# fp8 attention of an eight-layer kernel: k, v and q projected apart, and another order on TensorE, ScalarE and VectorE

## The chip, the cores and the metric

One core of a Trainium2 chip. Its engines run their own instruction streams in order and meet through semaphores: TensorE (PE: matmuls and transposes, results in PSUM), ScalarE (ACT: functions, copies out of PSUM), VectorE (DVE: elementwise work and reductions), GpSimd (POOL, which works in SBUF here) and SyncE (SP, which issues the transfers). The metric is the device time of one execution in microseconds; lower is better.

## The reference, cut to what matters

The model is four pairs of a gated attention and a gated feed-forward layer on x (8 batches, 128 tokens, 256 features), with a context of the same shape. The change touches the second attention, `L1_xattn`: 16 query heads and 8 key heads of 128, once over the tokens and once over the context.

```python
ln_out = _ln(hidden_states, ln_w, ln_b)
q = _fp8_linear_pertensor(ln_out, wq, wq_scale, q_in_scale).reshape(b, s, g, hpg, d)
q = _ln(q, qln_w, qln_b)
k = _fp8_linear_pertensor(ln_out, wk, wk_scale, k_in_scale).reshape(b, s, g, d)
k = _ln(k, kln_w, kln_b)
v = _fp8_linear_pertensor(ln_out, wv, wv_scale, v_in_scale).reshape(b, s, g, d)
core = _gqa(q, k, v).reshape(b, s, nh * d)
qx = _fp8_linear_pertensor(ln_out, wqx, wqx_scale, qx_in_scale).reshape(b, s, g, hpg, d)
qx = _ln(qx, qxln_w, qxln_b)
kvx = jnp.einsum('bsi,oi->bso', cond, w_kv_x)
kx, vx = jnp.split(kvx, 2, axis=-1)
kx = _ln(kx.reshape(b, sc, g, d), kxln_w, kxln_b)
xout = _gqa(qx, kx, vx.reshape(b, sc, g, d)).reshape(b, s, nh * d)
catq = _div_clamp_fp8(jnp.concatenate([core, xout], axis=-1), proj_smooth)
return jnp.einsum('bsi,oi->bso', catq, wproj) * (proj_in_scale * proj_w_scale)
```

`_fp8_linear_pertensor` divides its input by a scale for each feature, clamps it, rounds it to fp8 and multiplies by the weights; `_gqa` is softmax(q k / sqrt(128)) v.

## The kernel before

The program runs the eight layers one after the other, each as one stream of instructions per engine. x stays in SBUF. The stage of interest (names that begin with C_) works on two batches at a time (g = 0, 1) in four steps. A **unit** is one batch and one of eight rounds r; a round is four query heads, rounds 0 to 3 over the tokens, 4 to 7 over the context. The 16 units of a step are u = 2 r + g. Two rounds share four key heads, so the units with u % 4 = 0 or 1 bring k and v (`brings_kv`). For r < 4 k and v come from the quantised input with weights split in two f16 parts (`project_split`, 4 matmuls of 512 columns), for r >= 4 from the context in f32 (`project`, 2 matmuls, each issued as two). q is always split.

The work is laid out by hand as a pipeline of **slots**: `C_slots` emits for slot n, for each entry (lag, stage) of an engine's list in the order of that list, that stage of unit n - lag, and then `extra`. `C_pipeline` emits slots 0 to 5, a hardware loop over three steps of slots 6 to 21, and once more slots 6 to 21, of which those from 16 on only finish units. Slots 16 to 21 of a step already take units 0 to 5 of the next one. The lists at L1214, L1251, L1324 and L1447 are the order of each engine.

What the stages of a unit do, in the order of its data:

- TensorE `projections`: k and v where due, then q, each into its own bank of PSUM (KBANK, VBANK, QBANK). k waits until the previous k is normalised (C_kn), v until the previous one is copied (C_v), q until the previous q is normalised (C_qn).
- ScalarE `squares_k`, `squares_q` (four squares with a sum each, then `variance` at L1267); GpSimd `deviations` (a power, L1227); VectorE `normed_k`, `normed_q` (L1153, L1158).
- TensorE `turn_k`, `turn_q` (four transposes each, both into TBANK, so they alternate with the copies `k_T`, `q_T` of ScalarE).
- TensorE `scores`, which wait for q's copy and for the previous exponentials (one bank, SBANK); VectorE `largest` (L1164); ScalarE `exps` (L1312); VectorE `probabilities` (L1171, L1172); TensorE `turn_p`; ScalarE `p_T` (L1318).
- ScalarE `v_out` copies v out of VBANK; TensorE `weigh` multiplies v by the turned p (L1424), after VectorE has read the previous result.
- VectorE `rounded` (L1180 to L1182, rounding to fp8 by L1113 to L1115), GpSimd `unshifted` (L1238), TensorE `out` (output projection, L1436).

Beside the units, `extra` of VectorE carries the inputs of the next step: `activations` quantises one batch's normalised input for one of four uses (n = 0 q, 1 qx, 2 k, 3 v; L1142 to L1146 and L1113 to L1120), in slots 11 to 16 and in 17 and 18; `norm_stats`, `again`, `twice_normed` in slots 6, 7 and 8 normalise the next two batches. TensorE turns them at the end of slot 10. A flag is a semaphore whose value says how many units have passed; `follow` takes over the semaphore of an earlier stage, where it stopped.

Of the kernel before, what the change touches and what calls it, by code (L numbers as in the profile page):

```python
# [29 lines left out]
G = 2  # L30
# [55 lines left out]
def program(nc, t, out, layers=8):  # L86

    with ExitStack() as ctx:
# [35 lines left out]
        ctxT = sb("ctxT", [P, G, KC, P])  # L124
# [462 lines left out]
        B_had = flag("B_had")  # L587
# [344 lines left out]
        C_vq = flag("C_vq", ROUNDS)  # L932
# [189 lines left out]
        def C_vector(dve, ch):  # L1122
# [61 lines left out]
            def extra(ch, i, n):  # L1184
                if n == UNITS + DEPTH - 1:
                    dve.wait_ge(C_out.sem, C_out.at(i))
                    for g in range(G):
                        add_to_x(dve, ch, i * G + g, PS[:, OUTBANK, g * D:(g + 1) * D], out_scale[:])
                if last_step(i):
                    return  # L1190
                if 1 <= n % UNITS <= G:
                    activations(ch, n % UNITS - 1, 1)
                if n == DEPTH:
                    norm_stats(ch, i + 1)
                if n == DEPTH + 1:
                    again(ch, i + 1)
                if n == DEPTH + 2:
                    twice_normed(ch, i + 1)
                if 11 <= n < 17:
                    m, g = divmod(n - 11, G)  # L1200
                    if m == 0:
                        dve.wait_ge(xT_ready.sem, xT_ready.at(i + 1, g))
                    activations(ch, g, (2, 3, 0)[m])
# [10 lines left out]
            C_pipeline(dve, ch, first, [(2, largest), (3, probabilities), (5, rounded), (0, normed_k), (0, normed_q)], extra)  # L1214
# [38 lines left out]
        def C_scalar(act, ch):  # L1253
# [25 lines left out]
            def squares_q(ch, i, u):  # L1279
                g, r = unit(u)  # L1280
                act.wait_ge(C_vq.sem, C_vq.nth(i, u))
# [5 lines left out]
            def v_out(ch, i, u):  # L1287
                if brings_kv(u):
                    g, r = unit(u)
                    nc.scalar.activation(flat(C_[g]["v"][:, (r // 2) % 2]), PS[:, VBANK, :], ACT.Copy,  # L1290
# [33 lines left out]
            C_pipeline(act, ch, lambda ch: feature_major(0), [(0, squares_k), (0, squares_q), (2, exps), (1, k_T), (0, v_out), (1, q_T), (3, p_T)],  # L1324
                       extra)

        def C_tensor(pe):
# [22 lines left out]
            def projections(ch, i, u):  # L1350
                g, r = unit(u)
                cross, quad, half = r // 4, (r // 2) % 2, r % 2
                x_of = lambda n: (lambda k: C_[g]["xs"][:, n, k, :])
                ctx_of = lambda k: ctxT[:, g, k, :]
                if r == 0:
                    pe.wait_ge(C_xs.sem, C_xs.nth(i, 8 * (u // UNITS) + 4 + g))
                if r == 4:
                    pe.wait_ge(C_xs.sem, C_xs.nth(i, 6 + g))
                    ctx_loaded(pe, i, g)
                if half == 0:  # L1360
                    if u:
                        pe.wait_ge(C_kn.sem, C_kn.nth(i, kv_at(u) - 1))
                        pe.wait_ge(C_v.sem, C_v.nth(i, kv_at(u) - 1))
                    if u == 12 and not last_step(i):
                        pe.wait_ge(xT_ready.sem, xT_ready.at(i + 1, G - 1))
                    if cross:
                        project(KBANK, ctx_of, wC["kx"], 512 * quad).then_inc(C_k.sem, 1)
                        last = project(VBANK, ctx_of, wC["vx"], 512 * quad)
                        if quad:
                            last.then_inc(ctx_read[g], 1)  # L1370
                    else:
                        project_split(KBANK, x_of(2), "k", 512 * quad).then_inc(C_k.sem, 1)
                        project_split(VBANK, x_of(3), "v", 512 * quad)
                if u:
                    pe.wait_ge(C_qn.sem, C_qn.nth(i, u - 1))
                project_split(QBANK, x_of(cross), "qx" if cross else "q", 1024 * quad + 512 * half).then_inc(C_vq.sem, 1)
# [65 lines left out]
            def extra(ch, i, n):  # L1442
                if n == 10 and not last_step(i):
# [4 lines left out]
                       [(2, scores), (0, projections), (1, turn_k), (3, turn_p), (6, out), (1, turn_q), (4, weigh)], extra)  # L1448
# [1531 lines left out]
```

## Time and profile before

| | us |
|---|---|
| median of 3 runs | 1937.25 |
| lowest, highest | 1935.76, 1951.46 |
| profiled execution | 1931.56 |
| its span, first to last instruction | 1929.8 |
| TensorE, VectorE, ScalarE, GpSimd busy | 1464.8, 1213.7, 977.1, 241.7 |
| mean granted TensorE clock | 0.823 |

The rows come from one profiled execution. Busy time counts an engine's instructions, not its waits. Each row of a time line is one instruction or a run of equal ones; in brackets stands how long the engine had sat idle before it and which instruction ended that. A granted clock of 1.00 is 2.4 GHz and 0.50 is 1.2 GHz. Matmuls are pipelined, so the distance from one start to the next says more than a duration.

### The profile page before, as it was taken

To read this page: it belongs to the slowest core of one execution; us is meant where nothing else is said; L and a number is where in the kernel's file an instruction comes from. 1 tells how busy PE (TensorE), PEld (TensorE's weight loads), DVE (VectorE), ACT (ScalarE), POOL (GpSimd) and SP (SyncE) were. 2 spreads that over 40 slices of the span, in tenths; PEclk is the share of its full clock that TensorE was granted. 3 is DMA by queue.
4 is the path that set the end of the run, shared out by engine and by line. 5 is a ranking of instruction groups with operands and counts; after the bars stand their busy time and mean duration, and the time that the engine had idled before them with its cause. 6 is when DMAs were issued, how large, how long until landed. Compare 5 with 4: busy or idle time off the path is not lost.

```text
span 1929.8 us, 27060 instructions
## 1 busy us (share of the span) xinstructions
PE 1464.8 (76%) x9102; PEld 1011.3 (52%) x9122; DVE 1213.7 (63%) x2725; ACT 977.1 (51%) x2871; POOL 241.7 (13%) x323
## 2 busy tenths in 40 slices
PE   5764554477777777786699998648888898988786
PEld 4652432255555555554577776324444445766564
DVE  4677887567868778756233322569898897662442
ACT  2543765466666766764244543137777776222111
POOL 0000000133333333332000000000000000000000
PEclk8876786699999999999699999756666555996889
DMA  5102001000000000000500000000000001000000
GB/s 227 78 3 88 0 1 41 6 1 6 1 1 6 0 0 6 1 1 1 230 1 1 0 0 0 14 3 1 1 0 0 0 1 44 1 0 0 1 0 22
DMA packets 13572, 37.97 MB, mean 20 GB/s; under 512 B 2201, under 2 KB 8866, under 8 KB 10802
## 3 DMA queue, kind: packets, MB, share of 16 engines
q1 hardware_dynamic: 13490, 36.99, 5.0%
q8 instruction: 38, 0.62, 0.1%
q14 instruction: 44, 0.36, 0.1%
HBM read 35.94 MB, written 1.05 MB: 19 GB/s over the span
## 4 chain that ended last, share of the span: by engine, by line
PE 48%; DVE 23%; issue 13%; ACT 10%; POOL 4%; DMA 1%; DVEq 0%; POOLq 0%; ACTq 0%; SPq 0%
PE PS L2120 4%; PE PS L2100 3%; PE PS L2732 3%; PE PS L1347 3%; DVE small L2240 3%; PE PS L1764 2%; PE PS L1404 2%; PE PS L1720 2%; POOL small L1227 2%; DVE work L2250 2%; ACT work L1312 2%; PE PS L1709 2%; PE PS L1699 2%; PE PS L1744 2%; POOL work L1238 2%
## 5 line engine op out<-in xcount | busy, mean ns | idle before, releaser
L2185 ACT ACTIVATE work<-PS,small 128x1024 f32<-128x1024 f32 x128 | 154.9, 1210 | 24.5 <-DVE small L2242 23.4
L2240 DVE TENSOR_REDUCE small<-PS 128x1 f32<-128x1024 f32 x128 | 156.3, 1221 | 15.9 <-PE PS L2100 10.7
L2120 PE MATMUL PS<-ident_b,work 128*128 128x128 bf16 x1024 | 121.9, 294 | 42.8 <-DVE work L2250 36.6
L206 POOL TENSOR_TENSOR rstd<-moments,eps 128x1 f32<-128x1 f32 x56 | 12.5, 223 | 1091.9 <-DVE moments L186 1091.9
L1227 POOL TENSOR_TENSOR small<-small,minus_half 128x4 f32<-128x4 f32 x96 | 102.3, 1066 | 347.4 <-ACT small L1267 346.8
L2100 PE MATMUL PS<-early,work 64*128 64x512 bf16 x256 | 120.1, 567 | 4.7 <-ACT work L2185 3.0
L1347 PE MATMUL PS<-late 128*128 128x512 f16 x384 | 104.0, 412 | 19.9 <-DVE late L1120 17.6
L2120 PEld LDWEIGHTS PS<-ident_b,work 128*128 128x128 bf16 x1024 | 91.8, 133 | 48.2 <-DVE work L2250 37.1
L2178 ACT COPY work<-PS 128x512 f32<-128x512 f32 x128 | 75.1, 586 | 66.2 <-PE PS L2120 66.1
L1283 ACT ACTIVATE work<-PS 128x128 f32<-128x128 f32 x256 | 67.4, 278 | 76.3 <-PE PS L1347 76.3
L1404 PE MATMUL PS<-work 128*128 128x128 f32 x512 | 75.2, 292 | 29.1 <-ACT work L1305 28.8
L1164 DVE TENSOR_REDUCE small<-PS 128x4 f32<-128x512 f32 x64 | 44.0, 687 | 84.3 <-PE PS L1404 84.3
L2250 DVE TENSOR_SCALAR work<-work 128x1024 bf16<-128x1024 f32 x128 | 87.5, 684 | 7.1 <-ACT work L2185 5.0
L1312 ACT ACTIVATE work<-PS,small 128x128 f32<-128x128 f32 x256 | 89.3, 357 | 4.5 <-DVE small L1165 4.5
L1404 PEld LDWEIGHTS PS<-work 128*128 128x128 f32 x512 | 66.3, 199 | 47.5 <-ACT work L1305 45.0
L2136 PEld LDWEIGHTS PS<-work 128*128 128x128 bf16 x1024 | 36.9, 104 | 96.8 <-ACT work L2178 83.9
L1565 DVE TENSOR_TENSOR late<-late,PS 128x512 f32<-128x512 f32 x16 | 11.0, 687 | 117.1 <-ACT late L1625 117.1
L1394 PE MATMUL PS<-ident,work 128*128 128x128 f32 x256 | 41.1, 284 | 56.2 <-ACT work L1298 56.2
L1275 ACT ACTIVATE work<-PS 128x128 f32<-128x128 f32 x128 | 33.7, 278 | 94.8 <-PE PS L1347 51.0
L1238 POOL TENSOR_TENSOR work<-work 128x512 f16<-128x512 f32 x64 | 74.1, 1158 | 36.2 <-DVE work L1115 36.2
L1424 PE MATMUL PS<-work 128*128 128x256 f32 x256 | 68.9, 392 | 11.6 <-DVE work L1115 11.6
L1347 PEld LDWEIGHTS PS<-late 128*128 128x128 f16 x384 | 39.8, 105 | 69.7 <-issue 28.2
(399 smaller groups left out, 3641.7 us busy)
## 6 DMA issues: line engine op xcount, KB each, us to landing
late<-in_C_proj SPq DMA_DIRECT2D x1, 4096.0 KB, 12.2
ctxT<-in_ctxT SPq DMA_DIRECT2D x24, 128.0 KB, 2.5
late<-in_C_q SPq DMA_DIRECT2D x1, 2048.0 KB, 9.0
late<-in_C_qx SPq DMA_DIRECT2D x1, 2048.0 KB, 13.2
late<-in_F_w SPq DMA_DIRECT2D x2, 1024.0 KB
late<-in_B_gate SPq DMA_DIRECT2D x1, 1024.0 KB, 8.3
late<-in_B_up SPq DMA_DIRECT2D x1, 1024.0 KB, 10.3
late<-in_B_down SPq DMA_DIRECT2D x1, 1024.0 KB, 12.3
```

The lines of the kernel that those rows point to most:

```text
L1227: return nc.gpsimd.tensor_tensor(rs, rs, minus_half[:, 0:4], ALU.pow)
L1238: nc.gpsimd.tensor_tensor(c["cat"], c["t"], c["m"], ALU.subtract).then_inc(C_cat.sem, 1)
L1312: last = nc.scalar.activation(C_[g]["p"][:, h, :], PS[:, SBANK, h * P:(h + 1) * P], ACT.Exp, scale=DC ** -0.5, bias=small[:, g, 8 + h:9 + ...
L1347: last = nc.tensor.matmul(PS[:, n, :], src(k), w, start=k == 0 and part == 0, stop=k == KC - 1 and part == 1)
L1404: last = nc.tensor.matmul(PS[:, SBANK, h * P:(h + 1) * P], c["qT"][:, h, :], c["kT"][:, 2 * (r % 2) + h // 2, :], start=True, stop=True)
L1424: last = nc.tensor.matmul(PS[:, OBANK, h * D:(h + 1) * D], c["v"][:, (r // 2) % 2, 2 * (r % 2) + h, :], c["pT"][:, 2 * h:2 * h + 2, :].rea ...
L2100: last = nc.tensor.matmul(bank(g, 2 + n), E_[g]["qT"][r, h // 2, :], E_kT[r, h // 2, n * 512:(n + 1) * 512], start=True, stop=True)
L2120: last = nc.tensor.transpose(bank(g, 1).bitcast(BF16)[:, b * P:(b + 1) * P], E_[g]["pb"][:, b * P:(b + 1) * P], ident_b[:])
L2178: nc.scalar.copy(E_[g]["pT"].rearrange("p a b -> p (a b)").bitcast(F32), bank(g, 1)).then_inc(E_pT.sem, 1)
L2185: nc.scalar.activation(E_[g]["e"], banks(g, 2), ACT.Exp, scale=small[:, g, h:h + 1], bias=small[:, g, 48 + h:49 + h], accum_out=small[:, g ...
L2240: ch.link(nc.vector.tensor_reduce(small[:, g, 80:81], banks(g, 2), AX.X, ALU.max))
L2250: nc.vector.tensor_scalar(E_[g]["pb"], E_[g]["e"], MAGIC, MAGIC - 1.0, ALU.add, ALU.subtract).then_inc(E_pb.sem, 1)
```

## The change

TensorE's `projections` becomes three stages, `project_k`, `project_q` and `project_v`, with the same matmuls. Their places in the list: k and q first of the slot, then k's turning, then the scores (which were first), p's turning, and v. v gets a flag of its own (C_vp, on the semaphore of B_had), for which `v_out` now waits; for the last v of a batch from the context it waits for the flag `ctx_read`. On ScalarE k's copy goes ahead of the exponentials. On VectorE the maxima go from first to third place, behind probabilities and rounding, and the quantised inputs from the end of the slot to between the normalised k and q.

```diff
-        B_had = flag("B_had")
+        B_had = flag("B_had_C_vp")
...
-        C_vq = flag("C_vq", ROUNDS)
+        C_qp = flag("C_qp", ROUNDS)
+        C_vp = follow(B_had, ROUNDS // 2 - 1)
...
                 if last_step(i):
                     return
-                if 1 <= n % UNITS <= G:
-                    activations(ch, n % UNITS - 1, 1)
                 if n == DEPTH:
                     norm_stats(ch, i + 1)
                 if n == DEPTH + 1:
                     again(ch, i + 1)
                 if n == DEPTH + 2:
                     twice_normed(ch, i + 1)
+
+            def inputs(ch, i, n):
+                if last_step(i):
+                    return
+                if 1 <= n % UNITS <= G:
+                    activations(ch, n % UNITS - 1, 1)
                 if 11 <= n < 17:
                     m, g = divmod(n - 11, G)
...
-            C_pipeline(dve, ch, first, [(2, largest), (3, probabilities), (5, rounded), (0, normed_k), (0, normed_q)], extra)
+            C_pipeline(dve, ch, first, [(3, probabilities), (5, rounded), (2, largest), (0, normed_k), (0, inputs), (0, normed_q)], extra)
...
             def squares_q(ch, i, u):
                 g, r = unit(u)
-                act.wait_ge(C_vq.sem, C_vq.nth(i, u))
+                act.wait_ge(C_qp.sem, C_qp.nth(i, u))
...
             def v_out(ch, i, u):
                 if brings_kv(u):
                     g, r = unit(u)
+                    if r >= 6:
+                        act.wait_ge(ctx_read[g], i + (ctx_base[0] + 2 + u // UNITS))
+                    else:
+                        n = kv_at(u)
+                        act.wait_ge(C_vp.sem, C_vp.nth(i, n % 8 + 6 * (n // 8)))
...
-            C_pipeline(act, ch, lambda ch: feature_major(0), [(0, squares_k), (0, squares_q), (2, exps), (1, k_T), (0, v_out), (1, q_T), (3, p_T)],
+            C_pipeline(act, ch, lambda ch: feature_major(0), [(0, squares_k), (0, squares_q), (1, k_T), (2, exps), (0, v_out), (1, q_T), (3, p_T)],
                        extra)
...
-            def projections(ch, i, u):
+            def place(u):
                 g, r = unit(u)
-                cross, quad, half = r // 4, (r // 2) % 2, r % 2
                 x_of = lambda n: (lambda k: C_[g]["xs"][:, n, k, :])
-                ctx_of = lambda k: ctxT[:, g, k, :]
+                return g, r, r // 4, (r // 2) % 2, x_of, lambda k: ctxT[:, g, k, :]
+
+            def project_k(ch, i, u):
+                g, r, cross, quad, x_of, ctx_of = place(u)
+                if not brings_kv(u):
+                    return
                 if r == 0:
                     pe.wait_ge(C_xs.sem, C_xs.nth(i, 8 * (u // UNITS) + 4 + g))
                 if r == 4:
+                    ctx_loaded(pe, i, g)
+                if u:
+                    pe.wait_ge(C_kn.sem, C_kn.nth(i, kv_at(u) - 1))
+                if cross:
+                    project(KBANK, ctx_of, wC["kx"], 512 * quad).then_inc(C_k.sem, 1)
+                else:
+                    project_split(KBANK, x_of(2), "k", 512 * quad).then_inc(C_k.sem, 1)
+
+            def project_q(ch, i, u):
+                g, r, cross, quad, x_of, ctx_of = place(u)
+                if r == 4:
                     pe.wait_ge(C_xs.sem, C_xs.nth(i, 6 + g))
...
                 if u:
                     pe.wait_ge(C_qn.sem, C_qn.nth(i, u - 1))
-                project_split(QBANK, x_of(cross), "qx" if cross else "q", 1024 * quad + 512 * half).then_inc(C_vq.sem, 1)
+                project_split(QBANK, x_of(cross), "qx" if cross else "q", 1024 * quad + 512 * (r % 2)).then_inc(C_qp.sem, 1)
+
+            def project_v(ch, i, u):
+                g, r, cross, quad, x_of, ctx_of = place(u)
+                if not brings_kv(u):
+                    return
+                if u:
+                    pe.wait_ge(C_v.sem, C_v.nth(i, kv_at(u) - 1))
+                if u == 12 and not last_step(i):
+                    pe.wait_ge(xT_ready.sem, xT_ready.at(i + 1, G - 1))
+                if cross and quad:
+                    project(VBANK, ctx_of, wC["vx"], 512 * quad).then_inc(ctx_read[g], 1)
+                elif cross:
+                    project(VBANK, ctx_of, wC["vx"], 512 * quad).then_inc(C_vp.sem, 1)
+                else:
+                    project_split(VBANK, x_of(3), "v", 512 * quad).then_inc(C_vp.sem, 1)
...
             C_pipeline(pe, None, lambda ch: turn_x(0),
-                       [(2, scores), (0, projections), (1, turn_k), (3, turn_p), (6, out), (1, turn_q), (4, weigh)], extra)
+                       [(0, project_k), (0, project_q), (1, turn_k), (2, scores), (3, turn_p), (0, project_v), (6, out), (1, turn_q), (4, weigh)], extra)
```

## Rows read from the trace of the kernel before

**Rows 1.** Windows of the stage: start:end, length, busy us of each engine, granted clock.
```profile
342.50:405.30 62.80, 32.30 (x140) 18.51 (x141) 30.81 (x85) 32.87 (x142) 11.33 (x11) 0.74 0.00 1
541.13:582.55 41.42, 32.93 (x192) 22.86 (x193) 28.35 (x64) 26.97 (x119) 16.31 (x20) 1.00 0.00 1
582.55:650.73 68.18, 52.65 (x307) 35.49 (x305) 56.62 (x137) 45.34 (x201) 21.96 (x20) 0.97 0.01 4
650.73:674.18 23.45, 18.39 (x117) 12.96 (x117) 16.95 (x38) 17.40 (x79) 8.85 (x8) 1.00 0.00 0
807.18:895.09 87.91, 68.64 (x400) 47.70 (x401) 52.47 (x113) 56.01 (x246) 27.24 (x25) 1.00 0.00 1
```

**Rows 2.** Costliest groups of the page: busy, mean ns, idle before, releaser.
```profile
L1164 DVE TENSOR_REDUCE small<-PS 128x4 f32<-128x512 f32 x64 | 44.0, 687 | 84.3 <-PE PS L1404 84.3
```

**Rows 3.** Time line of TensorE in slot 9: start, duration, instruction, idle before.
```profile
564.31 1.16 PE L1404 MATMUL PS<-work 128*128 128x128 f32 x8 [1.59 <-ACT work L1305]
565.31 3.60 PE L1339 MATMUL PS<-late,ctxT 128*128 128x512 f32 x8
568.75 1.03 PE L1347 MATMUL PS<-late 128*128 128x512 f16 x4
569.61 0.60 PE L1384 MATMUL PS<-ident,work 128*128 128x128 f32 x4
570.04 0.60 PE L1413 MATMUL PS<-ident,work 128*128 128x128 f32 x4
570.48 1.04 PE L1436 MATMUL PS<-late,work 128*128 128x256 f16 x8
573.49 0.66 PE L1394 MATMUL PS<-ident,work 128*128 128x128 f32 x4 [1.97 <-ACT work L1298]
573.99 1.03 PE L1424 MATMUL PS<-work 128*128 128x256 f32 x4
```

**Rows 4.** Time line of ScalarE in the same slot.
```profile
569.81 0.28 ACT L1283 ACTIVATE work<-PS 128x128 f32<-128x128 f32 x1 [1.01 <-PE PS L1347]
...
571.28 0.35 ACT L1312 ACTIVATE work<-PS,small 128x128 f32<-128x128 f32 x1
...
572.65 0.79 ACT L1298 ACTIVATE work<-PS,C_col 128x512 f32<-128x512 f32 x1
573.32 0.61 ACT L1290 ACTIVATE work<-PS 128x512 f32<-128x512 f32 x1
...
574.87 0.58 ACT L1318 COPY work<-PS 128x512 f32<-128x512 f32 x1
```

**Rows 5.** Time line of VectorE in slot 12, with an input made.
```profile
591.00 0.68 DVE L1164 TENSOR_REDUCE small<-PS 128x4 f32<-128x512 f32 x1
...
592.00 0.69 DVE L1172 TENSOR_TENSOR work<-work,small 128x512 f32<-128x512 f32 x1
592.61 0.68 DVE L1180 TENSOR_TENSOR work<-PS,C_inv 128x512 f32<-128x512 f32 x1
...
595.06 0.68 DVE L1153 TENSOR_TENSOR work<-PS,small 128x512 f32<-128x512 f32 x1
596.89 0.69 DVE L1158 TENSOR_TENSOR work<-PS,small 128x512 f32<-128x512 f32 x1 [1.14 <-POOL small L1227]
597.50 0.76 DVE L1142 TENSOR_SCALAR work<-xT,C_inv 128x128 f32<-128x128 f32 x2
...
599.95 0.68 DVE L1164 TENSOR_REDUCE small<-PS 128x4 f32<-128x512 f32 x1
```

**Rows 6.** TensorE's projections in slot 17, and the window after their start.
```profile
633.95 4.26 PE L1347 MATMUL PS<-late 128*128 128x512 f16 x12 [0.64 <-DVE late L1120]
...
634.00:635.00 1.00, 1.00 (x3) 0.35 (x4) 0.93 (x4) 0.00 (x0) 0.00 (x0) 0.50 0.00 0
```

**Rows 7.** GpSimd and VectorE side by side near the stage's end.
```profile
900.40 1.16 POOL L1238 TENSOR_TENSOR work<-work 128x512 f16<-128x512 f32 x1 [5.16 <-DVE work L1115]
...
900.44 1.66 DVE L1172 TENSOR_TENSOR work<-work,small 128x512 f32<-128x512 f32 x1
```

## What the change will do to the time

> **What bounds the kernel now.** I read the page first, then the windows of the fp8 attention stage, then the time lines of TensorE, ScalarE and VectorE in a few of its slots. The change touches this stage alone: about 342 to 916 us of the span of 1929.8 us. It is a pipeline of slots. From 541.13 to 674.18 us one loop step (16 slots, two batches) takes 41.42 + 68.18 + 23.45 = 133.05 us [rows 1]: 8.3 us a slot. No engine is full: by the sums over the three windows TensorE is busy for 104.0 us of it, VectorE for 101.9, ScalarE for 89.7. The stage is bound by waits in a ring, and the reader should look for who stands behind whom. The page names the largest one on VectorE: the maxima wait 84.3 us in all for the scores [rows 2].
>
> One slot shows the ring. TensorE starts the scores at 564.31, k and v at 565.31, q at 568.75, and then waits 1.97 us at 573.49 for ScalarE before it can turn q [rows 3]. ScalarE could start the squares of q only at 569.81 after a wait of 1.01 us; it then does its exponentials (571.28), k's copy (572.65), v's copy (573.32), and the copy of the turned q last, just ahead of p's copy at 574.87 [rows 4]. The next scores wait for that copy, and the next projections stand behind those scores. So a slot is scores + projections + squares + exponentials + copies + turn, one after the other, on two engines in alternation: 10.7 us there. VectorE meanwhile waits, 1.14 us for q's deviations at 596.89 for instance [rows 5].
>
> **Prices, from start to start at the full clock.** TensorE [rows 3]: scores 1.00, q projection 0.86, a turning 0.43 to 0.50, output projection and weighing 1.04 and 1.03 at most. That is 4.9 us for a slot without k and v. k and v cost 3.44 more from the f32 context (half for each), and by the q price 1.7 more from the split weights; the slots after one with k turn k for 0.43. ScalarE [rows 4]: squares with variance 1.47, exponentials 1.37, a scaled copy 0.67, the p copy 0.58; so 4.1 us, and 2.1 more with k and v, 0.7 more where k is copied. VectorE [rows 5]: maxima and probabilities 1.61 (591.00 to 592.61), rounding 2.45 (592.61 to 595.06), a normalised k or q 0.61, one batch's quantised input 2.45 (597.50 to 599.95). So 4.7 us without k, 5.3 with it, 7.1 and 7.7 where an input is made.
>
> **What the change does, part by part.** (a) The v projection goes behind the scores and the turning of p. The 1.72 us of it no longer stand between k and q, and squares of q start that much earlier. ScalarE's v copy now waits for an own flag; behind it stand the copies of q and p, but v is projected well before the exponentials end (5 us into the slot against 6), so I cost the flag at nothing; without that cover it costs the 0.5 us copy. (b) k and q projections go ahead of the scores of the unit two before. TensorE no longer waits for the previous slot's last q copy before projecting; k may even start before the previous q is normalised. (c) k's copy goes ahead of the exponentials on ScalarE, so k's turn ends before them, the turning of q need not wait (1.97 us at 573.49 goes), and q's copy follows the exponentials at once. (d) VectorE takes probabilities and rounding first and the maxima third, so it has work while TensorE makes the scores; (e) its inputs sit between the normalised k and q, where it waited 1.14 us. Inputs are also ready earlier, so the projections at 633.95 wait less than the 0.64 us shown [rows 6]. No instruction is added or taken away, no DMA moves; only the waits can change.
>
> The new ring: exponentials 1.37, probabilities 0.8, rounding 2.45, maxima 0.9, then exponentials of the next unit, with some 0.15 for handing over: 5.7 us. Normalising fits under the exponentials. Every slot takes the longest of this ring and the three engine sums:
> - Eight slots of 16 with inputs (now 68.18 us): VectorE, 4 x 7.1 + 4 x 7.7 = 59.4. TensorE's 8.3 and 8.7 in two of them is worked off from the k projections that start early.
> - The other eight (now 64.87): two with no k or v 5.7 each (11.4); two that carry the next step's normalisation, 2 x 4.7 + 3.8 = 13.1, the 3.8 being VectorE's busy 28.35 in the first window of rows 1 less 24.6 for its five slots' own work; two with the f32 context, on TensorE, 8.3 less 1.7 for k started early, and 8.7 (15.3); two with split k and v, on ScalarE 6.1 and 6.8 (12.9). Sum 52.7.
>
> That gives 112.1 us a step before two frictions.
>
> *Collisions of VectorE and GpSimd.* At 900.44 VectorE's multiply of p takes 1.66 us while GpSimd's subtraction runs from 900.40, against 0.69 alone [rows 7, 5]: 0.97 lost. The new order puts other VectorE work beside that subtraction. Below: 0; above: once in each slot, 15.5 us a step. In the hand schedule the subtraction mostly meets reads of PSUM (maxima, normalised q) and only in slots with inputs other work, so I take 0.3 us in eight slots, 2.4.
> The Trainium skill (SBUF — State Buffer, Who interferes with whom) has the shared port pair as an exclusive lock against which a VectorE operation with two inputs in SBUF waits in full; by its rule, alone, each unit has two such operations that may lose. The row agrees in kind.
>
> *TensorE's clock.* At 634 us the granted clock is at 0.50, 1.2 GHz, after a wait of 0.64 us; the 12 matmuls there take 4.26 us against 12 x 0.215 = 2.6 at 2.4 GHz [rows 6, 3], so a fall costs about 1.6. In slots with inputs TensorE will have 4.9 us of work in 7.1, and its idle time will lie in one piece, so I expect falls there: below none, above one in each of eight slots, 12 us a step. I take two, 3 us: the fall now seen is there, and two kinds of slots are looser than it.
>
> Step: 112.1 + 2.4 + 3 = 117.5, saving 15.6.
>
> **The sum.** Of the two steady loop steps the one from 541.13 is taken for both; they save 31.2. The first loop step (405.30 to 541.13, 135.8 us) saves 1 more, 16.6. The last part has 11 slots without inputs in 87.91 us [rows 1]: three of 5.7 and twice (8.3 less 0.8 for k ahead, 8.7, 5.7, 5.7) make 17.1 + 55.2 = 72.3, saving 15.6. The start (62.8 us up to 405.30, at a granted clock of 0.74 [rows 1]) fills the pipeline: 0 to 10, I take 5. Together 68.4. Against the profiled execution's 1931.56 us (span 1929.8 and 1.8 around it) this makes 1863; the median of the runs shown stands 5.7 above it, so 1869. The stages before and behind are not touched; the next stage's weights are asked for when this one ends (916 us), earlier now with it.
>
> **The rivals.**
> 1. *Frictions are near nothing* (no more falls of the clock than now, no collisions): step 112 to 114, some 4.5 less in three steps, and the start saves 10: about 1850. For it: k projections fill some idle time. Against: the idle time in one piece.
> 2. *The slots with inputs give nothing back*: falls of the clock in each, so they stay at 68 and only the other eight gain. Step 68.2 + 52.7 = 120.9, or with half of the latter's gain also lost, 127. Savings 3 x 6 to 12 + 15.6: 1886 to 1904. For it: TensorE's share in these slots sinks to two thirds, and it falls now already in the most idle one. Against: 1.6 us per fall partly lies beside VectorE's work.
> By the Trainium skill (TensorE: Matmul & The Clock Gate, HAM oscillation) idle gaps between bursts put the array back at half rate, each burst then starting cold; that rule is for this rival, and the row at 634 us agrees.
> 3. *The other side: collisions on VectorE become the bound.* Place: the multiply of p and the sum in the rounding, both SBUF with SBUF, against GpSimd's subtraction and powers. Price up to 2 x 0.97 us for each of the 16 units of a step. At full price a step is 112.1 + 3 + 31 = 146, slower by 13; three steps and the last part (72.3 + 21, against 87.9) bring the kernel to some 1980. It decides from about 1.1 us lost per slot ((133.05 - 115.1) / 16). For it: VectorE is the longest engine now. Against: at 592.00 the multiply has its 0.69 [rows 5], and nothing keeps GpSimd off it there either.
> 4. *The change does not do what it says*: scores now stand behind a q projection that waits for the previous normalised q. If this wait sits where the old one sat, nothing is gained: about 1937. The chain is q normalised - projection 0.86 - k turned 0.43 - scores 1.0 and 0.2 to land - maxima 0.9 - k 0.6 - inputs 2.45 - q 0.61: 7.1 us, less than 8.3 and beside VectorE's own 4.1 us. So it binds nothing alone.
>
> **How the numbers follow.** Forecast (1856 to 1882): 0.47. Rival 1 (1838 to 1856): 0.2. Rival 2 (1882 to 1912): 0.2. Rival 4 and a smaller gain (1912 to 1956): 0.09. Rival 3: 0.04. The range 1838 to 1912 leaves out 0.13. One per cent is 19.4 us, about what a measurement of this kernel can tell from no change: faster (below 1918) 0.88, within 1% 0.08, slower 0.04. Forecast 1869.
>
> **What the profile of after would show.** A steady step of 112 to 121 us, taken from the scores of one slot to those 16 later. No wait of the turning of q for k's copy (1.97 us before). VectorE's wait for the scores well below the 84.3 us; probabilities and rounding start right after the exponentials or the normalised q. VectorE over 85% busy in the slots with inputs. The granted clock: one to three stretches at 0.5 a step. The multiply of p longer than 0.69 on the mean if collisions matter. The forecast is wrong if the clock stays low through several slots, or if ScalarE, not VectorE, turns out to stand between two exponentials.

## The result, and the profile after

The changed kernel takes 1856.74 us (median of 4 runs, 1852.25 to 1864.4) against 1936.51 us; the ratio is 0.9584, 95% interval 0.9543 to 0.9624: 4.2% faster. The forecast was 1869 in a range of 1838 to 1912, and faster. The profiled execution has a span of 1850.5 us, 79.3 less than before.

The windows of the stage after, in the columns of [rows 1]: the start from the first scores to those of slot 6, the three parts of the second loop step, and the last part. (In [rows 1] the first window begins at 342.50 us, ahead of the first scores; from those, at 368.95 us, to slot 6 the kernel before took 36.35 us.)

```profile
370.84:396.19 25.35, 20.34 (x109) 14.16 (x109) 15.81 (x36) 21.87 (x97) 7.44 (x7) 0.88 0.00 1
510.12:542.69 32.57, 30.75 (x190) 22.55 (x189) 27.80 (x65) 26.23 (x119) 16.84 (x20) 1.00 0.00 1
542.69:606.55 63.86, 51.63 (x306) 37.84 (x305) 60.28 (x141) 45.30 (x201) 22.99 (x20) 0.95 0.01 4
606.55:625.42 18.87, 18.32 (x122) 13.11 (x120) 16.36 (x35) 16.87 (x78) 9.48 (x8) 1.00 0.00 1
741.95:810.19 68.24, 63.77 (x395) 46.69 (x393) 53.64 (x113) 54.21 (x245) 29.05 (x25) 1.00 0.00 1
```

The second loop step takes 115.3 us, where it took 133.05 [rows 1]; the first takes 113.9 (135.8), the third 116.5 (133.0). The eight slots with inputs went from 68.18 to 63.86, the other eight from 64.87 to 51.44. VectorE is busy for 60.28 of 63.86 us in the former; TensorE is busy for 49.07 of 51.44 in the latter, and for 63.77 of 68.24 in the last part. From slot 6 to the last scores it is now mostly one engine or the other that sets the pace, and no longer a wait. The start (the busiest engine, ScalarE, at 86%) and the 20.6 us after the last scores are not of that kind.

The group that answers to [rows 2], VectorE's maxima over the whole span: idle before it 12.9 us, where it was 84.3.

```profile
L1165 DVE TENSOR_REDUCE small<-PS 128x4 f32<-128x512 f32 x64 | 43.8, 685 | 12.9 <-PE PS L1429 12.9
```

TensorE's time line from the scores of slot 8 into slot 9 (with [rows 3]): scores (L1429), p's turning (L1438), v (the first L1349), output projection (L1461), q's turning (L1419), weighing (L1449), then slot 9's k (the second L1349), q (L1357) and k's turning (L1409).

```profile
522.83 1.07 PE L1429 MATMUL PS<-work 128*128 128x128 f32 x8
523.96 0.66 PE L1438 MATMUL PS<-ident,work 128*128 128x128 f32 x4
524.45 1.88 PE L1349 MATMUL PS<-late,ctxT 128*128 128x512 f32 x4
526.17 1.04 PE L1461 MATMUL PS<-late,work 128*128 128x256 f16 x8
527.04 0.60 PE L1419 MATMUL PS<-ident,work 128*128 128x128 f32 x4
527.48 1.03 PE L1449 MATMUL PS<-work 128*128 128x256 f32 x4
528.34 1.88 PE L1349 MATMUL PS<-late,ctxT 128*128 128x512 f32 x4
530.06 1.03 PE L1357 MATMUL PS<-late 128*128 128x512 f16 x4
530.92 0.60 PE L1409 MATMUL PS<-ident,work 128*128 128x128 f32 x4
```

No row has a wait in brackets; q's turning, which waited 1.97 us for k's copy at 573.49 [rows 3], starts the moment the output projection leaves. VectorE in slot 14, with an input made (with [rows 5]):

```profile
566.15 0.68 DVE L1181 TENSOR_TENSOR work<-PS,C_inv 128x512 f32<-128x512 f32 x1
...
568.59 0.68 DVE L1165 TENSOR_REDUCE small<-PS 128x4 f32<-128x512 f32 x1
569.31 0.17 DVE L1166 TENSOR_SCALAR small<-small 128x4 f32<-128x4 f32 x1
569.39 1.37 DVE L1143 TENSOR_SCALAR work<-xT,C_inv 128x128 f32<-128x128 f32 x2
...
572.45 0.68 DVE L1159 TENSOR_TENSOR work<-PS,small 128x512 f32<-128x512 f32 x1
573.05 0.17 DVE L1172 RECIPROCAL small<-small 128x4 f32<-128x4 f32 x1
573.25 0.69 DVE L1173 TENSOR_TENSOR work<-work,small 128x512 f32<-128x512 f32 x1
```

Rounding, maxima, inputs, normalised q and the next probabilities follow each other without a gap. The two instructions of L1143, which scale the input, take 1.37 us here, 0.76 at 597.50 in [rows 5]; the section on GpSimd's subtraction says why.

The stage ends at 830.78 us, where it ended at 916.29: 85.5 us earlier. The other layers give 6.2 of it back: from there to the end 1019.7 us against 1013.5, with the same TensorE and VectorE instructions, at a granted clock of 0.76 against 0.77 and TensorE busy for 850 us against 842.

### The profile page after: what moved, and what is told of

Same layout as the page of the kernel before. It is cut to its first block, busy times and chain, and to the rows that moved or that the text cites. A ratio compares the mean times of both kernels' runs of the same rounds, so it can differ in the third digit from the quotient of the medians.

```text
span 1850.5 us, 27056 instructions
## 1 busy us (share of the span) xinstructions
PE 1457.0 (79%) x9102; PEld 1021.9 (55%) x9122; DVE 1222.8 (66%) x2725; ACT 971.0 (52%) x2871; POOL 248.8 (13%) x323
## 4 chain that ended last, share of the span: by engine, by line
PE 49%; DVE 32%; ACT 8%; issue 7%; POOL 1%; DMA 1%; DVEq 0%; ACTq 0%; SPq 0%; POOLq 0%; another core or an unknown queue 0%
PE PS L2145 4%; PE PS L2125 4%; PE PS L2757 4%; DVE small L2265 3%; DVE work L1116 2%; PE PS L1789 2%; PE PS L1745 2%; DVE work L2275 2%; PE PS L1734 2%; PE PS L1724 2%; PE PS L1769 2%; PE PS L1349 2%; PE PS L354 2%; PE PS L2792 2%; DVE small L1165 1%
## 5 line engine op out<-in xcount | busy, mean ns | idle before, releaser
L1357 PE MATMUL PS<-late 128*128 128x512 f16 x384 | 101.4, 395 | 57.9 <-DVE work L1159 33.9
L1232 POOL TENSOR_TENSOR small<-small,minus_half 128x4 f32<-128x4 f32 x96 | 108.7, 1133 | 265.1 <-ACT small L1272 264.9
L1322 ACT ACTIVATE work<-PS,small 128x128 f32<-128x128 f32 x256 | 90.2, 364 | 51.9 <-DVE small L1166 51.9
L1357 PEld LDWEIGHTS PS<-late 128*128 128x128 f16 x384 | 35.8, 100 | 110.2 <-DVE work L1159 46.1
L1288 ACT ACTIVATE work<-PS 128x128 f32<-128x128 f32 x256 | 67.0, 280 | 34.6 <-PE PS L1357 31.7
L1429 PE MATMUL PS<-work 128*128 128x128 f32 x512 | 75.5, 295 | 4.9 <-ACT work L1315 4.8
L1429 PEld LDWEIGHTS PS<-work 128*128 128x128 f32 x512 | 70.6, 209 | 13.8 <-ACT work L1315 10.5
L1243 POOL TENSOR_TENSOR work<-work 128x512 f16<-128x512 f32 x64 | 74.2, 1159 | 20.1 <-DVE work L1116 20.1
L1449 PE MATMUL PS<-work 128*128 128x256 f32 x256 | 66.6, 383 | 3.7 <-DVE work L1116 3.6
L2757 PE MATMUL PS<-work,late 128*128 128x256 f32 x256 | 66.2, 424 | 2.7 <-ACT work L2732 2.7
L1461 PE MATMUL PS<-late,work 128*128 128x256 f16 x480 | 64.9, 278 | 2.9 <-POOL work L1243 2.8
L1679 ACT ACTIVATE work<-PS,small 128x128 f32<-128x128 f32 x128 | 45.2, 365 | 37.7 <-DVE small L1600 37.7
```

The lines of the kernel that those rows point to most:

```text
L1232: return nc.gpsimd.tensor_tensor(rs, rs, minus_half[:, 0:4], ALU.pow)
L1243: nc.gpsimd.tensor_tensor(c["cat"], c["t"], c["m"], ALU.subtract).then_inc(C_cat.sem, 1)
L1322: last = nc.scalar.activation(C_[g]["p"][:, h, :], PS[:, SBANK, h * P:(h + 1) * P], ACT.Exp, scale=DC ** -0.5, bias=small[:, g, 8 + h:9 + ...
L1357: last = nc.tensor.matmul(PS[:, n, :], src(k), w, start=k == 0 and part == 0, stop=k == KC - 1 and part == 1)
L1429: last = nc.tensor.matmul(PS[:, SBANK, h * P:(h + 1) * P], c["qT"][:, h, :], c["kT"][:, 2 * (r % 2) + h // 2, :], start=True, stop=True)
L2757: last = nc.tensor.matmul(PS[:, bank_ + c % 2, n * D:(n + 1) * D], wH[name][:, k, at:at + P], H_rT[:, k, :], start=k == 0, stop=k == KC - 1)
```

## The experiments

Each was timed beside the kernel before on its own chip; ratios are to that. "Step" is the second loop step in the trace, from the scores of its slot 6 to those of the next; the changed kernel has 115.3. A second trace of the changed kernel (`after_again`) has steps of 115.5, 116.6 and 116.4 us against 113.9, 115.3 and 116.5 here: a difference of some 1.5 us between two single steps is within what the same kernel shows.

### One order undone at a time

VectorE's maxima first again (`u_dve`):

```diff
-            C_pipeline(dve, ch, first, [(3, probabilities), (5, rounded), (2, largest), (0, normed_k), (0, inputs), (0, normed_q)], extra)
+            C_pipeline(dve, ch, first, [(2, largest), (3, probabilities), (5, rounded), (0, normed_k), (0, inputs), (0, normed_q)], extra)
```

> The changed kernel with VectorE's maxima back in first place, ahead of probabilities and rounding; all else as changed. Ring theory (exponentials, probabilities, rounding, maxima set the slot, and VectorE must have work while TensorE makes q projection and scores): VectorE now waits 2.1 to 2.5 us a slot for q projection 0.86, k's turning 0.43, scores 1.0 and 0.2, before it may do anything. Slots with inputs 7.1 + 2.2 to 7.7 + 2.4, the others 6.8 and more: a step of 135 to 142 us against 115.3, time 1925 to 1950. Rival (the gain is TensorE's, from v off the way of q; VectorE's order is minor): step 115 to 120, time 1857 to 1872.

1991.2 us, ratio 1.0293 (1.0248 to 1.0337): slower than the kernel before, with a step of 155.7 us. The groups by line over that step, where VectorE waits for the scores in each of 16 slots, 46.8 us in all (for 0.7 us in the changed kernel's step):

```profile
L1165 DVE TENSOR_REDUCE small<-PS 128x4 f32<-128x512 f32 x16 | 11.1, 692 | 46.8 <-PE PS L1429 46.8
```

The direction is the ring theory's; the size is larger, by 14 us. Its other half stands in the longest waits of that step (engine and line, whom it waited for, total, times, longest): TensorE's p turning (L1438) waits for the probabilities, which stand behind the maxima, and everything behind the turning on TensorE waits too. I had counted only VectorE's side. The granted clock also fell in this step, to 0.96, 0.91 and 0.86 in its three parts, and TensorE was busy for 111.2 us where the changed kernel has 100.7; how much of the 14 us is that was not told apart.

```profile
DVE small L1165 <- PE PS L1429: 46.8, 16, 4.4
POOL work L1243 <- DVE work L1116: 35.3, 15, 4.1
PEld PS L1438 <- DVE work L1173: 30.1, 15, 2.1
PE PS L1438 <- DVE work L1173: 28.8, 16, 1.9
```

ScalarE's k copy behind the exponentials again (`u_act`):

```diff
-            C_pipeline(act, ch, lambda ch: feature_major(0), [(0, squares_k), (0, squares_q), (1, k_T), (2, exps), (0, v_out), (1, q_T), (3, p_T)],
+            C_pipeline(act, ch, lambda ch: feature_major(0), [(0, squares_k), (0, squares_q), (2, exps), (1, k_T), (0, v_out), (1, q_T), (3, p_T)],
```

> The changed kernel with k's copy back behind the exponentials on ScalarE; all else as changed. Ring theory: after slots with k, q's turning waits for the copy until 0.7 us after the exponentials, q's copy and the scores follow 1.3 us later than now; VectorE has 3.3 us of other work meanwhile, so only 0 to 1.6 us are lost in some six slots without inputs: step 116 to 123 us, time 1860 to 1880. Rival (the copy ahead of the exponentials is what took the 1.97 us wait away, so it returns in eight slots): step 125 to 131, time 1885 to 1905.

1885.2 us, ratio 0.9734 (0.9695 to 0.9773), step 122.2. The wait of q's turning for k's copy is back eight times a step, and in full. First the kernel before, then this one (in the changed kernel 1.6 us in 2 waits):

```profile
PE PS L1394 <- ACT work L1298: 12.8, 8, 2.0
PE PS L1419 <- ACT work L1308: 14.2, 8, 3.1
```

Yet the step grows by 6.9 only, within the ring theory's range (the time is 5 us above its range, at the rival's edge). So about half of the wait is covered by other work; that VectorE's is what covers it is the theory's reading.

TensorE's scores first again (`u_scores`):

```diff
-                       [(0, project_k), (0, project_q), (1, turn_k), (2, scores), (3, turn_p), (0, project_v), (6, out), (1, turn_q), (4, weigh)], extra)
+                       [(2, scores), (0, project_k), (0, project_q), (1, turn_k), (3, turn_p), (0, project_v), (6, out), (1, turn_q), (4, weigh)], extra)
```

> The changed kernel with the scores back in first place on TensorE, ahead of k and q projections; v stays late, ScalarE and VectorE as changed. Ring theory: k and q are projected 1.0 us and the wait for q's copy later, their squares too; slots with k and v get 0.8 to 1.5 us longer, those without stay at the ring: step 118 to 124 us, time 1865 to 1885. Rival (next unit's k and q first is the main gain): step 126 to 132, time 1890 to 1910.

1897.8 us, ratio 0.9809 (0.9766 to 0.9851), step 125.5: the step lies between the two expectations, the time in the rival's. All of the 10.2 us lost are in the slots without inputs (36.98 + 25.38 = 62.4 us against 51.4); the others take 63.15. So next unit's k and q first is worth more than I gave it. The wait that comes back is that of the scores, first in the slot, for the copy of the turned q, which hardly occurs in the changed kernel (0.9 us a step on the weight loads):

```profile
PE PS L1429 <- ACT work L1315: 18.4, 16, 1.9
```

The inputs behind the normalised q again (`u_inputs`), and the same kernel once more beside the changed one (`u_inputs_again`, `after_again`):

```diff
-            C_pipeline(dve, ch, first, [(3, probabilities), (5, rounded), (2, largest), (0, normed_k), (0, inputs), (0, normed_q)], extra)
+            C_pipeline(dve, ch, first, [(3, probabilities), (5, rounded), (2, largest), (0, normed_k), (0, normed_q), (0, inputs)], extra)
```

> The changed kernel with VectorE's inputs behind the normalised q again. Theory A (VectorE's sum bounds the slots with inputs, its waits for q's deviations are gone anyway): q is normalised 2.45 us earlier, TensorE's idle time of 2.2 to 2.7 us moves but stays; step 113 to 117, time 1850 to 1862, perhaps fewer falls of the clock. Theory B (the inputs cover the wait for q's deviations, 1.1 to 1.9 us in slots with k): that wait returns in four slots: step 119 to 122, time 1868 to 1880.

> The changed kernel with the inputs behind the normalised q, once more and beside the changed kernel itself. If the gain of some 13 us seen on another chip is the order's, this is 6 to 15 us below the changed kernel (1841 to 1851) with steps of 113.5 to 115; if it was the chip's or the granted clock's in other layers, the two agree within 4 us.

> The changed kernel unaltered, on the chip of the three runs beside it, to have their common yardstick: ratio to the kernel before 0.955 to 0.962, a step of 113.5 to 116.5 us.

The first time: 1843.9 us, ratio 0.9513 (0.947 to 0.9556), step 114.75. Side by side, five rounds: 1853.0 (1838.05 to 1857.95), ratio 0.9587 (0.9565 to 0.961), against 1856.4 and 0.9607 (0.9592 to 0.9622) for the changed kernel; steps 115.3 and 116.6. In both traces the stage ends some 7 us earlier than in the changed kernel's (824.07 against 830.78 on another chip, 824.98 against 832.52 on the same one), but the layers behind it took 1022.8 us in one trace and 1011.3 in the other. So this part of the change brings nothing; by the traces it costs the stage some 7 us, while the times side by side differ by 3.4 us with overlapping intervals. Theory A's steps held (its time did the second time; the first time lay below its range): the wait for q's deviations that the inputs were to cover, 9.8 us a step in the kernel before, is only 4.3 us with the inputs last and 2.7 with them ahead.

### One part alone on the kernel before

Only v late on TensorE (`b_vlate`): the list of `u_scores`, with the old lists on ScalarE and VectorE and the inputs last.

> The kernel before with one part of the change: v's projection behind the scores and p's turning, with its flag; the scores still first on TensorE, ScalarE, VectorE and the inputs in the old order. Ring theory: the old ring (scores, projections, squares, exponentials, copies, turn) gets shorter by the v projection, 1.7 us in four slots and 0.9 in four: step 133.05 - 10 = 121 to 125, time 1900 to 1915. Rival (v was hidden beside waits, the order of the three engines is all): step 131 to 134, time 1930 to 1940.

1910.2 us, ratio 0.9881 (0.9863 to 0.9899), step 126.4 (7 less than before, and 1.4 above the expected range; the time lies within it). By itself this move gives 25 us, a third of the whole gain of 80. That v late is also needed in the changed kernel was not tested: no run there moves v back alone.

The changed TensorE list alone (`b_te`), the other engines as before:

> The changed TensorE list (k and q first, scores fourth, v late) with ScalarE's and VectorE's lists and the inputs of the kernel before. Since VectorE with the maxima first and the changed TensorE list alone took a step of 155.7 us, the ring theory, with VectorE behind TensorE's scores and p's turning behind VectorE's probabilities, expects 150 to 160 here too, time 1975 to 2005. Rival (the long step of that run came from the new order of ScalarE or of the inputs): step 115 to 135, time below 1940.

1954.6 us, ratio 1.0092 (1.0071 to 1.0113), step 138.2. It is slower than the kernel before, by 0.9% with an interval clear of 1, but step and time lie between the two expectations. VectorE waits 33.3 us a step for the scores instead of 46.8:

```profile
L1165 DVE TENSOR_REDUCE small<-PS 128x4 f32<-128x512 f32 x16 | 11.1, 691 | 33.3 <-PE PS L1429 33.3
```

Of the 17.5 us between the steps of `u_dve` and `b_te`, 14.9 are in the slots with inputs (86.0 against 71.1). That fits the inputs' place: here they stand behind the normalised q, so q projection and scores can run beside them. It is not shown, since k's copy has its old place here too and the granted clock in those slots is 0.98 against 0.91.

The orders need each other: k and q ahead of the scores costs 44 us with the old lists of VectorE and ScalarE and the inputs last (`b_vlate` to `b_te`, 1910.2 to 1954.6 on one chip), and brings 41 with the new ones (`u_scores` to the changed kernel, 1897.8 to 1856.7).

### The two frictions

TensorE kept busy (`clk`), the weighing repeated in six slots of the loop:

```diff
-            def weigh(ch, i, u):
+            def weigh(ch, i, u, again=0):
...
-                for h in range(2):
+                for h in [*range(2)] * (1 + again):
...
+            def weigh_slot(ch, i, u):
+                n = u + 4
+                weigh(ch, i, u, 0 if last_step(i) else {13: 1, 14: 2, 15: 2, 16: 1, 17: 1, 18: 2}.get(n, 0))
...
```

> The changed kernel with the weighing of slots 13 to 18 of the loop repeated, once in 13, 16 and 17, twice in 14, 15 and 18: the same matmuls write the same results again, in TensorE's idle time of 1.3 to 2.7 us before the next q projection. Theory A (falls of the granted clock cost about 1.6 us each, and come from this idle time): clock 0.98 or more in the slots with inputs, against 0.95, a step of 112 to 114 against 115.3 to 116.5, time 1847 to 1853. Theory B (VectorE is the bound there and hides the slower matmuls): the clock rises, the step stays at 115 to 117, time 1855 to 1860.

1857.8 us, ratio 0.9576 (0.9533 to 0.9619): no difference in time. The clock did rise, from 0.95 in the changed kernel's slots with inputs (above) to 1.00:

```profile
542.55:606.09 63.54, 56.09 (x341) 41.83 (x340) 60.52 (x141) 45.19 (x201) 23.03 (x20) 1.00 0.02 4
```

The three steps are 113.5, 115.0 and 115.0 us against 113.9, 115.3 and 116.5, or 115.5, 116.6 and 116.4 in the second trace: without falls of the clock a step is 0.3 to 2.0 us shorter, hardly more than the two traces of the changed kernel differ. In the changed kernel's step shown there are two such falls; a window of 1 us in each has a granted clock of 0.50:

```profile
582.00:583.00 1.00, 1.00 (x5) 0.91 (x4) 0.93 (x3) 0.97 (x7) 0.00 (x0) 0.50 0.00 0
599.50:600.50 1.00, 1.00 (x7) 1.00 (x7) 0.93 (x3) 0.97 (x6) 0.14 (x1) 0.50 0.00 0
```

This is nearer to theory B: VectorE, busy for 60.5 of the 63.5 us here, hides most of them. The steps lie at and just below its range, and the time in it, but the layers behind the stage took 1031 us in this trace, so that the times could not show 1 or 2 us a step in any case.

GpSimd's subtraction cut to a quarter (`nocol`):

```diff
-                nc.gpsimd.tensor_tensor(c["cat"], c["t"], c["m"], ALU.subtract).then_inc(C_cat.sem, 1)
+                nc.gpsimd.tensor_tensor(c["cat"][:, 0:1], c["t"][:, 0:1], c["m"][:, 0:1], ALU.subtract).then_inc(C_cat.sem, 1)
...
-                        last = nc.tensor.matmul(PS[:, OUTBANK, g * D:(g + 1) * D], C_[g]["cat"][:, h, :],
+                        last = nc.tensor.matmul(PS[:, OUTBANK, g * D:(g + 1) * D], C_[g]["cat"][:, 0, :],
```

> The changed kernel with GpSimd's subtraction done for one head of four; the output projection uses that head four times, so three quarters of the rounded result are left out. GpSimd's 1.16 us become some 0.4. Theory A (GpSimd's subtraction holds VectorE up by 3.4 us a step: mean of the bf16 maximum 308 ns against 272, input scaling 550 against 478, negated maxima 250 against 170): those means return to 272, 478 and 170 and the step is 112 to 113.5, time 1846 to 1852. Theory B (these delays fall into waits): means return, step 115 to 116, time 1854 to 1859.

The kernel leaves out three quarters of the rounded result, so only its time counts. 1839.9 us, ratio 0.9513 (0.9497 to 0.953), step 109.9: 5.4 less, twice the expected gain. The same groups of VectorE over one step of the changed kernel and of this one (mean ns behind the comma):

```profile
L1143 DVE TENSOR_SCALAR work<-xT,C_inv 128x128 f32<-128x128 f32 x16 | 8.2, 550 | 0.0
L1115 DVE TENSOR_SCALAR work<-work 128x512 bf16<-128x512 bf16 (+1 forms) x24 | 7.4, 308 | 0.8
L1166 DVE TENSOR_SCALAR small<-small 128x4 f32<-128x4 f32 x16 | 4.0, 250 | 0.6
```

```profile
L1115 DVE TENSOR_SCALAR work<-work 128x512 bf16<-128x512 bf16 (+1 forms) x24 | 6.7, 277 | 0.8
L1143 DVE TENSOR_SCALAR work<-xT,C_inv 128x128 f32<-128x128 f32 x16 | 4.9, 347 | 0.0
L1166 DVE TENSOR_SCALAR small<-small 128x4 f32<-128x4 f32 x16 | 2.7, 170 | 0.6
```

The three groups explain 5.3 us (3.3 + 0.7 + 1.3) of the 5.4. What the shorter GpSimd instruction brings by being early was not told apart.

How an instruction is held up stands in the changed kernel's trace, beside the rows of VectorE from 569.31 above. GpSimd's rows there:

```profile
568.20 1.35 POOL L1232 TENSOR_TENSOR small<-small,minus_half 128x4 f32<-128x4 f32 x1 [5.42 <-ACT small L1272]
569.51 1.17 POOL L1243 TENSOR_TENSOR work<-work 128x512 f16<-128x512 f32 x1
```

The subtraction (L1243) ends at 570.68, the second scaling, which had started under it, at 570.76. In this step all six scalings that are held up end 0.08 us after the subtraction does: they wait it out. The power of L1232 holds up nothing, neither the 128x4 instruction at 569.31 nor the sum of the rounding (L1116) elsewhere in the stage. The spread of the 16 scalings (min/median/max in ns), first in the changed kernel, then in the kernel before:

```profile
L1143 DVE TENSOR_SCALAR work<-xT,C_inv x16: 273/278/1185, 545.8 to 603.0; 128x128 f32<-128x128 f32 x16
L1142 DVE TENSOR_SCALAR work<-xT,C_inv x16: 273/418/805, 588.3 to 650.0; 128x128 f32<-128x128 f32 x16
```

Undisturbed one takes 273 ns, and a pair 0.47 us from start to end. The kernel before already lost time here, 3.3 us a step by the means (16 x (478 - 273) ns), and the 0.76 us that the forecast took for a pair held 0.29 of it. The changed kernel loses 6.6 us a step in the three groups (4.4 + 0.9 + 1.3, by their means against 273, 272 and 170 ns).

### Two versions beyond

`imp1`: the inputs last, and ScalarE multiplies by the inverse scales in the inputs' stead; VectorE clamps on both sides in one instruction. `imp2`: also the last two inputs in slots 20 and 21.

```diff
-                for k in range(KC):
-                    last = nc.vector.tensor_scalar(c["t_in"][:, k * P:(k + 1) * P], xT[:, k, g, :], inv[:, n * KC + k:n * KC + k + 1],
-                                                   448.0, ALU.mult, ALU.min)
-                ch.link(last)
-                ch.link(nc.vector.tensor_scalar(c["y_in"], c["t_in"], -448.0, None, ALU.max))
+                dve.wait_ge(C_tin.sem, C_tin.nth(i, j))
+                ch.link(nc.vector.tensor_scalar(c["y_in"], c["t_in"], 448.0, -448.0, ALU.min, ALU.max))
...
-            C_pipeline(dve, ch, first, [(3, probabilities), (5, rounded), (2, largest), (0, normed_k), (0, inputs), (0, normed_q)], extra)
+            C_pipeline(dve, ch, first, [(3, probabilities), (5, rounded), (2, largest), (0, normed_k), (0, normed_q), (0, inputs)], extra)
...
+                for k in range(KC):
+                    last = nc.scalar.activation(C_[g]["t_in"][:, k * P:(k + 1) * P], xT[:, k, g, :], ACT.Copy,
+                                                scale=inv[:, n * KC + k:n * KC + k + 1])
+                last.then_inc(C_tin.sem, 1)
...
```

> Inputs behind the normalised q, and ScalarE does the inputs' first step: it multiplies xT by the inverse scales (two copies of 128 columns, at the head of the slot), and VectorE's next instruction clamps on both sides. VectorE has two instructions of 0.35 to 0.7 us less in eight slots of a step. Theory A (VectorE's work bounds the slots with inputs, GpSimd's collisions with just these two instructions included): step 106 to 110 us, time 1820 to 1832. Theory B (ScalarE's 0.9 us more at the head of the slot delays squares and exponentials by as much): step 112 to 115, time 1836 to 1846.

> As the kernel with ScalarE's scaling, and the two inputs for the context's queries made in slots 20 and 21 in place of 17 and 18. Theory A (slots 17 and 18 are bound by VectorE, 20 and 21 by ScalarE with VectorE idle 0.8 to 1.5 us there): 1 to 3 us a step less than with the scaling alone, time 3 to 8 us less. Theory B (ScalarE, with 6.1 and 6.8 us of its own there, takes 0.9 more each and VectorE the rest): equal or up to 2 us a step more.

`imp1`: 1833.2 us (1826.4 to 1852.7), ratio 0.9497 (0.946 to 0.9533), beside 0.9607 for the changed kernel on the same chip. The step is 111.06, against 115.3 with the inputs last alone: 4.3 less, and step and time lie between the two expectations. With the inputs last the scaling seldom met GpSimd's subtraction (330 ns a piece in the mean), so only 0.66 us in each of eight slots were there to be had, some 5 in all. `imp2`: 1837.2 us, ratio 0.9511 (0.9496 to 0.9527), step 111.56: no gain, as theory B has it.

## Why the prediction was right

**The bound and the ring.** That the stage waited in a ring of alternating engines, and that the new order breaks it, is shown: undoing any of the three orders lengthens the step, by 6.9 to 40.4 us, and in each case the wait that comes back is the one named (maxima for scores, q's turning for k's copy, scores for q's copy with the projections behind them). The fourth part, the inputs' place, has no share in the gain, though the prediction lists it as part (e); and that v late, part (a), is in it rests on `b_vlate`, made from the kernel before.

**The slots with inputs.** Forecast 59.4 plus frictions 5.4 = 64.8 us, measured 63.86, VectorE busy 94% of it. Right in sum, wrong in its two frictions. The collisions cost 6.6 us a step, of which the forecast's prices held 2.3 unseen (eight pairs at 0.29): 4.3 on top of them and not 2.4. The clock cost 0.3 to 2.0 and not 3. That the errors offset each other is luck. The clock's term failed where it said that a slow matmul adds its delay: TensorE has that much slack beside VectorE. (The 1.6 us for a fall was also a little high: 2.6 counts twelve starts, the 4.26 runs to the end of the last matmul.) The collisions' term failed by their place: I let them meet the probabilities, but they fall on the input scaling, on one instruction of the rounding (L1115) and on the small instruction after the maxima. The Trainium skill (SBUF — State Buffer, Who interferes with whom) names `tensor_scalar` too among the instructions that can contend with GpSimd, and the three groups that grow here are of that kind; that the one in second place is held for the other's whole instruction, as it says, agrees with the 0.08 us above. The multiply of two SBUF inputs, which it names as well, is at 0.70 us in the mean here, since the order seldom puts it beside the subtraction.

**The other slots.** Forecast 52.7, measured 51.44. In the last part, 72.3 forecast and 68.24 measured, the step that failed is "every slot takes the longest": I gave each slot without k at least the ring's 5.7 us, but the first such slot behind those with k took 4.5 from scores to scores (5.0 at slot 6), and the one after it 5.7 to 6.4. My reading is that the ring's work had queued up beside the long slots; no run tests it. Over four slots the sum of the busiest engine counts: TensorE is busy for 93% of the last part.

**The sum.** Saved by the trace, expected in brackets: start, up to slot 6, 9.1 (5); first loop step 21.9 (16.6); second and third 17.8 and 16.5 (15.6 each); last part 19.7 (15.6). That is 85 against 68. Of the 17 us more than forecast the other layers, which I had put at nothing, gave 6.2 back. The median came out 12 us below the forecast.

**The rivals.** Rival 1's time (1850) is nearer to the measured 1856.7 than the forecast's 1869, but not for its reason: the frictions were there. Rival 2 fell: the slots with inputs gained 4.3 us a step, and with the clock at 1.00 hardly more. Rival 3 is right in kind; collisions stay at 0.4 us a slot, far from 1.1. Rival 4 fell for the whole change, but is what the change would be with VectorE's maxima left first: `u_dve` and, by 0.9%, `b_te` are slower than the kernel before. Its chain was judged at 7.1 us "beside VectorE's own"; with the maxima first it is not beside that work but ahead of it, 9.7 us a slot.

**Open.** Whether the inputs' place costs the kernel its 7 us in time as it does in the stage, and what moves the granted clock in the other layers (1011 to 1034 us in the traces of all kernels, for the same work), was not settled.

## What to carry to other kernels

In a software pipeline whose engines run in order, write down for each wait what stands behind it on the same engine: an order that is good on one engine (next unit's matmuls first) can cost more than it brings until the engine that reads the results has other work in front of its read. After such a change count per group of slots, not per slot, and by the sum of the busiest engine; work that goes to the engine which now bounds the stage, also time it loses to another engine, is then worth its full length, and a stall on any other engine is worth little.

## What the runs showed of the hardware that was not expected

VectorE's `tensor_scalar` instructions that start while GpSimd's 1.16 us subtraction runs are held until just after its end (0.08 us for the scalings), even a 128x4 one (170 ns undisturbed, 250 in the mean) and a 128x128 scaling (273 ns undisturbed, 1185 at most). GpSimd's powers, which run for 1.0 to 1.35 us, held up none of them. Cutting the subtraction to a quarter gave back 5.4 us a step. Two or three stretches of TensorE at 1.2 GHz in a step cost 0.3 to 2.0 us, because another engine bounds those slots. And the same work of the other layers took 1011 to 1034 us, with TensorE's busy time moving along (840 to 863 us), when only the stage ahead of them, or only the chip, had changed: a scatter of up to 23 us that a comparison of times alone would put down to the change.
